# A fused RWKV, attention and mixture-of-experts layer: a subtraction moves from GpSimd to VectorE, the softmax quotient is formed once per tile, the set-up is re-cut, and all order lists are new

## The reference, cut to what matters

```python
def _L0_attn_ref(x, Wk, Wr, Wo, time_decay, time_first):      # x is layer-normed
    k = einsum('btc,hc->bth', x, Wk); v = r = einsum('btc,hc->bth', x, Wr)
    y = wkv_scan(-exp(time_decay), time_first, k, v)          # stable recurrence over t
    return einsum('bth,ch->btc', sigmoid(r) * y, Wo)

def _L0_ffn_ref(x, ...):                                      # x is layer-normed
    h = _rmsnorm(x, gamma1)
    q  = (h @ Wq + bq).reshape(b, t, H, HD)                   # 16 heads of 32
    kv = ((h @ Wdown + bdown) @ Wup + bup).reshape(b, t, H, 2 * HD)
    att = softmax(einsum('bthd,btgd->bthg', q, k) / sqrt(HD)) # over the heads of one token
    out = einsum('bthg,btgd->bthd', att, v).reshape(b, t, D)
    x = x + (out @ Wo + bo)
    h2 = _rmsnorm(x, gamma2)
    gate = softmax(h2 @ Wg + bg)                              # 8 experts, dense
    return x + einsum('btd,edf,bte->btf', h2, We, gate)
```

## Time and profile before

| what | value |
|---|---|
| median of three runs | 2910.02 us (2909.48 to 2913.99) |
| profiled execution, its own time | 2906.95 us |
| its span, first to last instruction | 2905.1 us |
| mean granted TensorE clock | 0.978 |
| TensorE matmul busy | 2618.6 us, 90% |
| VectorE busy | 2453.4 us, 84% |
| ScalarE busy | 1522.6 us, 52% |
| GpSimd busy | 1006.4 us, 35% |

### The profile page before, as it was taken

One profiled execution on the slowest core, in us unless ns is written; L12 is line 12 of the kernel. 1 busy time (PEld: TensorE's weight loads), 2 busy tenths in 40 slices (PEclk: granted clock), 3 DMA queues, 4 the chain that ended last, 5 costly groups with the idle time before them and its releaser, 6 DMA issues.

```text
span 2905.1 us, 49052 instructions
## 1 busy us (share of the span) xinstructions
PE 2618.6 (90%) x18896; PEld 1579.7 (54%) x18896; DVE 2453.4 (84%) x4353; ACT 1522.6 (52%) x2783; POOL 1006.4 (35%) x970
## 2 busy tenths in 40 slices
PE   2447999999999999999999999999999999999899
PEld 2324555555556555555655555555555555565454
DVE  5688888889888888988888898888889888888853
ACT  5664555555555555555555555555555555554531
POOL 0354333334333333433333343333333333333320
PEclk9768999999999999999999999999999999999999
DMA  6011111111111101111110111111011111111110
GB/s 213 15 30 30 38 37 16 29 32 37 38 37 32 21 26 35 37 38 38 23 30 23 38 37 37 37 23 28 26 37 38 38 38 22 26 28 37 30 23 15
DMA packets 579083, 102.51 MB, mean 35 GB/s; under 512 B 547346, under 2 KB 547474, under 8 KB 578834
## 3 DMA queue, kind: packets, MB, share of 16 engines
q1 hardware_dynamic: 578852, 99.39, 16.5%
HBM read 48.49 MB, written 16.78 MB: 22 GB/s over the span
## 4 chain that ended last, share of the span: by engine, by line
PE 54%; DVE 32%; ACT 6%; issue 4%; POOL 2%; SPq 1%; DMA 0%; DVEq 0%; ACTq 0%; POOLq 0%
PE bank L1333 49%; DVE wkv L1134 4%; DVE ks L1219 3%; PE bank L1355 3%; DVE acc L1311 3%; DVE zz L1158 2%; DVE wkv L1123 2%; DVE e L1147 2%; DVE ev L1167 2%; DVE on L1253 2%; DVE zz L1130 2%; DVE mcol L1234 1%; DVE h2t L1096 1%; ACT ot L923 1%; DVE hrow L1225 1%
## 5 line engine op out<-in xcount | busy, mean ns | idle before, releaser
L1333 PE MATMUL bank<-w_e,h2t 128*128 128x512 f16 x6144 | 1392.8, 380 | 72.9 <-DVE acc L1311 52.6
L1333 PEld LDWEIGHTS bank<-w_e,h2t 128*128 128x128 f16 x6144 | 587.3, 98 | 754.6 <-DVE acc L1311 77.1
L1311 DVE SCALAR_TENSOR_TENSOR acc<-bank,gates,acc 128x512 f32<-128x512 f32 x512 | 376.6, 741 | 136.6 <-PE bank L1333 132.3
L727 POOL TENSOR_TENSOR pr<-pr 128x512 f16<-128x512 f32 x256 | 307.1, 1200 | 281.9 <-ACT pr L901 279.2
L899 ACT ACTIVATE pr<-bank,plog,col 128x512 f32<-128x512 f32 x256 | 197.1, 770 | 201.0 <-PE bank L1501 201.0
L1134 DVE TENSOR_TENSOR_SCAN wkv<-e,wkv 128x256 f32<-128x256 f32 x256 | 255.9, 1040 | 22.9 <-ACT e L827 19.6
L696 POOL TENSOR_TENSOR zz<-wkv,zz 128x512 f32<-128x512 f32 x64 | 106.7, 1667 | 432.2 <-DVE ev L1145 432.2
L1333 PE MATMUL bank<-w_o,xo 128*128 128x512 f16 x768 | 176.1, 387 | 49.7 <-DVE xo L1096 49.5
L1158 DVE RECIPROCAL zz<-zz 128x256 f32<-128x256 f32 x128 | 218.5, 1729 | 0.0
L901 ACT ACTIVATE pr<-bank,plog,col 128x512 f16<-128x512 f32 x256 | 197.0, 770 | 0.0
L1333 PE MATMUL bank<-xo,w_k 128*128 128x256 f16 x1536 | 175.6, 275 | 12.0 <-DVE xo L1096 12.0
(11 more groups left out here) (197 smaller groups left out, 4297.7 us busy)
## 6 DMA issues: line engine op xcount, KB each, us to landing
qs<-qo SPq DMA_DIRECT2D x384, 64.0 KB, 2.4
xk<-in_attn_x SPq DMA_DIRECT2D x32, 512.0 KB, 4.8
x<-in_attn_x SPq DMA_DIRECT2D x32, 512.0 KB, 3.9
result<-acc SPq DMA_DIRECT2D x32, 512.0 KB, 2.8
ks<-k SPq DMA_DIRECT2D x128, 64.0 KB, 2.4
w_e<-in_ffn_We SPq DMA_DIRECT2D x7, 1024.0 KB, 14.2
qs<-in_attn_Wk SPq DMA_DIRECT2D x1, 1024.0 KB, 5.8
ks<-in_attn_Wr SPq DMA_DIRECT2D x1, 1024.0 KB, 8.0
```

The costliest lines, as they stand in the source:

```text
L727: nc.gpsimd.tensor_tensor(pr16[:, 1, k % 2, :], pr[:, k % 2, :], pr16[:, 0, k % 2, :], ALU.subtract).then_inc(att_pool.sem, 1)
L1311: V.scalar_tensor_tensor(out=acc[:, s, :], in0=moe_bank[u % 2][:, :], scalar=gates[:, s, e:e + 1], in1=acc[:, s, :], op0=ALU.mult, op1=ALU ...
L1333: ins = nc.tensor.matmul(dst, left(a), right(b), start=(n == 0), stop=(n == last))
```

## The change

It has five parts.

1. The low half of the probabilities is formed by VectorE (`att_plo`) and no longer by GpSimd (`att_scores` of GpSimd is gone). Same operands, same shape, eight times a tile.
2. VectorE's `att_probs` only adds the two halves of a block's result, the column of sums included (33 columns a group, not 32). The reciprocal of all 32 sums and one multiplication of 128x1024 follow once per tile in `fin_back`, each behind a wait on the step before it.
3. In the set-up, the largest absolute values of `o1` and `o2` are found by ScalarE's `set_abs` and no longer by VectorE's `set_max`, and `set_max` for the small weights waits for the first two of them.
4. The loads are one step each in SyncE's list, and the turned weight blocks use six banks.
5. All lists are new.

```diff
-MAXED = ["k", "r", "o1", "q", "o2", "small", "experts"]
+MAXED = ["k", "r", "q", "small", "experts"]
+SUMMED = ["o1", "o2"] + [f"e{e}" for e in range(E)]
+TURN_BANKS = [0, 1, 4, 5, 6, 7]
...
 DVE_ORDER = [
-    ("mix_value", 1, 2), ("mix_scan", 1, 2), ("moe", 3, 4), ("mix_rec", 2, 2), ("moe", 4, 4), ("moe", 5, 4),
-    ("att_probs", 0, 3), ("att_probs", 1, 3), ("mix_rec", 3, 2), ("mix_gate", 1, 2), ("att_probs", 2, 3),
...
+    ("mix_gate", 1, 2), ("att_plo", 0, 3), ("moe", 4, 4), ("att_plo", 1, 3), ("mix_split", 1, 2), ("att_probs", 0, 3),
+    ("att_plo", 2, 3), ("att_probs", 1, 3), ("att_plo", 3, 3), ("att_probs", 2, 3), ("pre_stats", 0, 1),
...
-        on = sb("on", [P, G, HD])
+        on = sb("on", [P, G, HD + 1])
...
         def turned(n):
-            return bank[n % 2][:, :]
+            return bank[TURN_BANKS[n % len(TURN_BANKS)]][:, :]
...
@@ gpsimd
-            def att_scores(t, k):
-                pool.wait_ge(*att_act.done(t, "ex", 2 * k + 1))
-                if k >= 2:
-                    pool.wait_ge(*att_pe.done(t, f"PV{k - 2}"))
-                nc.gpsimd.tensor_tensor(pr16[:, 1, k % 2, :], pr[:, k % 2, :], pr16[:, 0, k % 2, :], ALU.subtract).then_inc(att_pool.sem, 1)
...
@@ scalar
             def set_abs(_, k):
-                name = f"e{k // 2}"
+                name = SUMMED[k // 2]
...
@@ vector
                 if name == "small":
+                    dve.wait_ge(summed, 2 * CB)
                     dve.wait_ge(smalls_in, 16 * 7)
...
                 elif name == "experts":
-                    dve.wait_ge(summed, E * CB)
+                    dve.wait_ge(summed, len(SUMMED) * CB)
...
+            def att_plo(t, k):
+                dve.wait_ge(*att_act.done(t, "ex", 2 * k + 1))
+                if k >= 2:
+                    dve.wait_ge(*att_pe.done(t, f"PV{k - 2}"))
+                V.tensor_tensor(pr16[:, 1, k % 2, :], pr[:, k % 2, :], pr16[:, 0, k % 2, :], ALU.subtract).then_inc(plo_dve.sem, 1)
+
             def att_probs(t, k):
                 pv = att_bank[ATT_BANK["PV", k]][:, 0:4 * VW].rearrange("p (g d) -> p g d", g=4)
-                og = on[:, 4 * k:4 * k + 4, :]
                 if k == 0 and t.back(1):
                     dve.wait_ge(*fin_dve.done(t.back(1), "ot"))
                 dve.wait_ge(*att_pe.done(t, f"PV{k}"))
-                V.reciprocal(rden[:, 4 * k:4 * k + 4], pv[:, :, HD]).then_inc(att_dve.sem, 1)
-                V.tensor_reduce(og, pv.rearrange("p g (l d) -> p g d l", l=2)[:, :, 0:HD, :], AX, ALU.add).then_inc(att_dve.sem, 1)
-                dve.wait_ge(*att_dve.done(t, "norm", 3 * k + 1))
-                V.tensor_tensor(og, og, rden[:, 4 * k:4 * k + 4].unsqueeze(2).to_broadcast([P, 4, HD]), ALU.mult).then_inc(att_dve.sem, 1)
+                V.tensor_reduce(on[:, 4 * k:4 * k + 4, :], pv.rearrange("p g (l d) -> p g d l", l=2), AX, ALU.add).then_inc(att_dve.sem, 1)
...
+                V.reciprocal(rden[:, :], on[:, :, HD]).then_inc(fin_dve.sem, 1)
+                dve.wait_ge(*fin_dve.done(t, "den"))
+                V.tensor_tensor(on[:, :, 0:HD], on[:, :, 0:HD], rden[:, :].unsqueeze(2).to_broadcast([P, G, HD]), ALU.mult).then_inc(fin_dve.sem, 1)
+                dve.wait_ge(*fin_dve.done(t, "quot"))
...
@@ tensor, set_turn
-                    if n >= 2:
-                        pe.wait_ge(lo_done, n - 1)
+                    if n >= len(TURN_BANKS):
+                        pe.wait_ge(lo_done, n - len(TURN_BANKS) + 1)
...
@@ tensor, att_probs
-                pe.wait_ge(*att_pool.done(t, "p_lo", k))
+                pe.wait_ge(*plo_dve.done(t, "p_lo", k))
```

More of the change, by code:

```diff
@@ new lines @@
+    ("mix_decay", 1, 1), ("pre_stats", 0, 2), ("att_latent", 0, 0), ("mix_sum", 1, 1), ("mix_value", 1, 1),
+    ("mix_scan", 1, 1), ("att_stack", 0, 0), ("mix_rec", 2, 1), ("att_vt", 0, 0), ("mix_rec", 3, 1),
+    ("pre_norm", 0, 2), ("att_vlo", 0, 0), ("att_max", 0, 0), ("att_max", 1, 0), ("att_max", 2, 0), ("att_max", 3, 0),
+    ("att_m", 0, 0), ("mix_gate", 1, 1), ("mix_split", 1, 1), ("att_plo", 0, 0), ("att_plo", 1, 0),
+    ("mix_project", 0, 1), ("att_probs", 0, 0), ("att_plo", 2, 0), ("att_probs", 1, 0), ("att_plo", 3, 0),
@@ new lines @@
+    ("pre_stats", 0, 2), ("att_plo", 0, 4), ("att_plo", 1, 4), ("att_probs", 0, 4), ("att_plo", 2, 4), ("moe", 5, 5),
+    ("pre_norm", 0, 2), ("att_probs", 1, 4), ("att_plo", 3, 4), ("att_probs", 2, 4), ("att_plo", 4, 4),
+    ("mix_gate", 1, 3), ("att_probs", 3, 4), ("att_plo", 5, 4), ("mix_split", 1, 3), ("att_probs", 4, 4),
+    ("att_plo", 6, 4), ("att_probs", 5, 4), ("att_plo", 7, 4), ("moe", 6, 5), ("moe", 7, 5), ("mix_project", 0, 3),
+    ("att_probs", 6, 4), ("att_probs", 7, 4), ("mix_turn", 0, 2), ("att_stats", 0, 3), ("moe", 8, 5),
@@ new lines @@
+    ("att_max", 1, 3), ("att_max", 2, 3), ("att_max", 3, 3), ("moe_gate", 0, 4), ("moe", 0, 4), ("att_m", 0, 3),
+    ("pre_stats", 0, 1), ("moe", 1, 4), ("mix_rec", 2, 2), ("mix_rec", 3, 2), ("moe", 2, 4), ("mix_gate", 1, 2),
+    ("att_plo", 0, 3), ("moe", 3, 4), ("att_plo", 1, 3), ("moe", 4, 4), ("mix_split", 1, 2), ("pre_norm", 0, 1),
+    ("att_probs", 0, 3), ("att_plo", 2, 3), ("att_probs", 1, 3), ("att_plo", 3, 3), ("att_probs", 2, 3),
+    ("att_plo", 4, 3), ("att_probs", 3, 3), ("att_plo", 5, 3), ("att_probs", 4, 3), ("att_plo", 6, 3), ("moe", 5, 4),
@@ new lines @@
+    ("att_probs", 5, 3), ("att_plo", 7, 3), ("moe", 6, 4), ("mix_project", 0, 2), ("mix_turn", 0, 1), ("moe", 7, 4),
+    ("att_probs", 6, 3), ("att_probs", 7, 3), ("att_stats", 0, 2), ("att_norm", 0, 2), ("fin_back", 0, 3),
+    ("mix_decay", 0, 1), ("moe", 8, 4), ("moe", 9, 4), ("mix_sum", 0, 1), ("mix_value", 0, 1), ("mix_scan", 0, 1),
+    ("mix_rec", 0, 1), ("att_turn", 0, 2), ("mix_rec", 1, 1), ("mix_gate", 0, 1), ("moe", 10, 4), ("moe", 11, 4),
+    ("mix_split", 0, 1), ("fin_project", 0, 3), ("mix_decay", 1, 1), ("att_latent", 0, 2), ("moe", 12, 4),
@@ new lines @@
+    ("moe", 13, 4), ("mix_sum", 1, 1), ("mix_value", 1, 1), ("mix_scan", 1, 1), ("moe", 14, 4), ("moe", 15, 4),
+    ("att_stack", 0, 2), ("att_vt", 0, 2), ("fin_turn2", 0, 3), ("att_vlo", 0, 2), ("att_max", 0, 2),
+    ("att_max", 1, 2), ("att_max", 2, 2), ("moe_gate", 0, 3), ("moe", 0, 3), ("att_max", 3, 2), ("att_m", 0, 2),
+    ("moe", 1, 3), ("mix_rec", 2, 1), ("moe", 2, 3), ("moe", 3, 3), ("mix_rec", 3, 1), ("mix_gate", 1, 1),
+    ("att_plo", 0, 2), ("att_plo", 1, 2), ("moe", 4, 3), ("moe", 5, 3), ("att_probs", 0, 2), ("att_plo", 2, 2),
@@ L388 @@
+    ("moe_store", 0, 1),
 ]
@@ L624, in set_masks, with set_experts @@
+            def set_experts(_, e):
+                load_weight(f"e{e}")
             def set_masks(_, k):
```

442 lines of the change are left out of this document (210 added, 232 removed).

## The result

The changed kernel takes 2813.01 us in the median of four runs (2812.12 to 2816.03), the kernel before 2910.86 beside it (2909.48 to 2913.99): ratio 0.9664, 95% interval 0.9647 to 0.9681. That is 98 us, more than twice the 41 forecast (2910.86 to 2870). The time is near the low end of the range, and near the 2820 of the first rival.

What follows compares the result with a forecast made beforehand. TensorE was taken to bound the body, working 80.8 of 85.05 us a tile. From 2907 us, 14 for the set-up and 22 for the body came off, 2871, predicted as 2870; range 2808 to 2903.

Steps and rivals of the forecast that it cites:

- the first rival: Body: TensorE nearly saturated; if the lists place VectorE right, 1.5 us idle a tile remain, 2820 us; chance 0.26.
- the body's sum of waits: Body: TensorE's waits fall from 4.35 to 3.5 us a tile, -0.85 a tile, -22 us over 26 tiles.
- acc: Body: TensorE's wait for additions to `acc` falls from 2.03 to 1.1 us a tile, about 1.0 before unit 14.
- h2t: Body: TensorE's wait for the second norm's low half rises from 0.77 to 1.3 us a tile, VectorE starting 0.5 late.
- Banks and xo: Body: waits for probability banks and the recurrence's low half, 0.81 + 0.51 before, become 0.9 us a tile.
- The rest: Body: TensorE's other waits stay at 0.2 us a tile.
- The floor: Body: TensorE's 80.8 us of work a tile stays unaltered; only its 4.3 us idle can be gained.
- VectorE's sum: VectorE per tile: +5.5 subtraction, -3.7 and +1.6 quotient, -4.6 less disturbance: -1.2 us, or +0.8 by the other bound.
- The relief of 4.6: VectorE beside the probabilities: instructions no longer stretched by GpSimd's L727 save 4.6 us a tile, bounds 2.6 and 4.6.
- Set-up and fill: Before the body: -14 us, first projection near 98 us; the fill's new order costed at nothing, could take back all 14.
- the six banks take no wait away: Set-up: six banks for turning remove no wait on the path, as turning is done before 46 us either way.
- The third: Rival, slower: subtraction in VectorE's in-order queue makes it late, 2933 us, or GpSimd disturbs it, 8 us a tile; 0.10 for both.

Runs made afterwards that it cites:

- old_lists_quot: Kernel before with its own lists and GpSimd's low halves, only the quotient formed once per tile instead of per block: 2859.4 us, ratio 0.9813.
- new_lists_only: Changed kernel with the probabilities' low halves back on GpSimd and the quotient per block, keeping new lists and set-up: 2843.2 us, ratio 0.9766.
- plo_pool: Changed kernel with only the probabilities' low halves back on GpSimd; new lists, quotient per tile and set-up stay: 2840.6 us, ratio 0.9758.
- old_lists_none: Kernel before with its own lists, the probabilities' low half a constant zero that no engine subtracts: 2832.6 us, ratio 0.9731.
- new_lists_none: Changed kernel with the probabilities' low half a constant zero that no engine subtracts: 2793.7 us, ratio 0.9596 to the kernel before.
- old_lists_both: Kernel before with its set-up and old lists, low-half subtractions inserted on VectorE and the quotient once per tile: 2966.6 us, ratio 1.0188.
- new_lists_extra: Changed kernel plus eight GpSimd subtractions a tile whose result nobody reads: 2862.7 us, ratio 0.9834 to the kernel before.

## Why the prediction was right or wrong

- **The step that failed** is the body's sum of waits, 3.5 us a tile left of 4.35, on a busy time of TensorE taken as fixed. It gave -0.85 a tile, -22 us; measured are -3.1 a tile, -80 us: 2.4 of idle and 0.7 of busy time. Every term of the 3.5 was too large. acc: 1.1 forecast, 18.2/23.2 tiles = 0.8 measured, at unit 14 as said. h2t: 1.3, measured 0.76, which is what it was before: the half microsecond of lateness did not come. Banks and xo: 0.9, measured 0, with 0.43 for the low half instead. The rest: 0.2, measured 0. Measured together: 1.98. With the set-up the forecast came to -36 us, the profiled execution measured -91.
- **What the runs show behind it.** Two things. In the old lists the reciprocal and the multiplication of each block made the bank and xo late: old_lists_quot clears both waits alone, for 52 us, and without them the two blocks that I counted as late, by 0.6 and 0.3 us, are not late at their banks. And the lists alone give 68 us with set-up, while I let them change VectorE's load by nothing ("Its load stays as it is, near 74 to 76 us"). They take 4.1 us a tile off it (new_lists_only). 3.1 of these are 8 scans by 0.138, 2 products e<-e,v by 0.522 and 2 ev<-e,ev by 0.465 us; after has 71.8. How much of the shorter waits comes from these shorter instructions and how much from the places of the pieces stays open: the load by itself doesn't decide, as plo_pool shows.
- **What bounds the kernel.** Right: TensorE's work bounds the body, and VectorE was late, not overloaded. The floor was wrong. I took 80.8 us of matmuls as fixed and 4.3 us idle as all there is to have. The idle time fell by 2.4 and the busy time by 0.7 (80.70 to 79.98) with the same matmuls. The busy time tends to go with the number of waits: by TensorE's waits of 500 to 2400 us some 6 a tile before (80.70), 4 in old_lists_none (80.19), 3 after (79.98), 2 in new_lists_none (79.79), which would be about 0.2 us for each wait beside the idle time that it shows. It is a correlation with exceptions: new_lists_only has 3 waits a tile too, and 80.37; and the profile models the ends of matmuls. One place fits it: where nothing is waited for, the transposes begin at 1479.19, 0.16 before the modelled end of the units ahead of them (1474.00 + 5.35); with the wait they don't overlap. No run tests it.
- **VectorE's sum.** For the subtraction, the quotient and the relief the sum was right: -1.2 forecast, -0.7 in old_lists_both. The relief of 4.6 was 4.2 in old_lists_none, but one part of it was put down to the wrong instruction: e<-e,v stood beside L709, not L727. The gate, 2 x 0.400 us, which the sum did not have, made up for most of it. The Trainium skill (GPSIMD Engine Reference, Key points) says that GpSimd shares its SBUF interfaces with VectorE and contends with VectorE instructions that have two SBUF inputs or run in a 2-port mode. The traces agree with it for two inputs, beside other GpSimd instructions than the one that I priced too. Without it the sum was +1.7.
- **Set-up and fill.** -14 forecast, -9 measured at tile 3. The first projection came 11.3 earlier, 3 us less than forecast, nearly all of it because ScalarE began with the experts 3.2 us later than I took. Another 2.4 went in the fill, inside the bound of "take back all 14". That the six banks take no wait away was wrong, by 9 us at the first product and about 2 at tile 3.
- **Rivals.** The first, at 0.26, is nearest in size (26 x 2.8 forecast, 26 x 3.1 measured) and in its mechanism, lists that place VectorE's pieces right. That its 2820 is so near is in part luck: the idle time fell by 2.4 and not by 2.8, the busy time, which it left alone, by 0.7, and the set-up gave 9 and not 14. What I held against it, long pieces of VectorE ahead of unit 14 and of h2t, costs 0.8 us each and no more. The third has its mechanism confirmed twice: the subtraction in VectorE's queue by old_lists_both, the disturbance by new_lists_extra; the lists are what keeps the kernel out of it.

How the gain divides, in one order of steps: lists and set-up 68 us (new_lists_only starts tile 3 at 287.97, 7.6 earlier than before, and its body gives 26 x 2.32 = 60, which only the lists can give), the quotient 3, the move 28. In another, the quotient 52 first. Neither division is the true one. Not settled either: how much of old_lists_none's 78 us is the shorter chain of a block and how much the disturbance, and how far better placed subtractions would repair old_lists_both.

## What to carry to other kernels

When work on GpSimd stretches VectorE, look up for each stretched instruction which GpSimd instruction ran beside it, and price an order by what it puts side by side, not only by the sum of durations. Judge removed stalls of TensorE by the period and not by the idle time alone: here the period fell by 3.1 us where the idle time fell by 2.4. When parts of a change attack the same lateness, time each alone in both orders before crediting any of them: the same edit was worth 52 us in the old lists and nothing that can be told apart (3 us and -1 us) in the new ones.

## What the runs showed of the hardware

- A VectorE instruction on 128x2 values with two SBUF inputs took 0.154 to 0.160 us alone and 1.107 to 1.109 while GpSimd worked on 128x512, whether GpSimd's result was used or not (L1112 after, L1130 in new_lists_extra). Even so small a one takes nearly as long as GpSimd's instruction then (1.16 to 1.20 us).
- VectorE's additions to acc, with one operand in a PSUM bank, took 0.735 to 0.747 us in the mean in every kernel, with GpSimd busy 465.5 or 724.8 of 1900 us (after, new_lists_extra), and never more than 0.754: they were not disturbed.
- Two tensor inputs are not needed to be disturbed. `zz<-e,ucol` reads one tensor and a column of scalars; before, it stood beside GpSimd's low halves of the keys (two took 1.42 us from 1433.90 on, GpSimd's L714 ran from 1433.49), after it does not. Stretch 500 to 2400 us of before, then of new_lists_only:

```profile
L1130 DVE TENSOR_SCALAR zz<-e,ucol 128x256 f32<-128x256 f32 x88 | 44.3, 544 | 1.6
```

```profile
L1137 DVE TENSOR_SCALAR zz<-e,ucol 128x256 f32<-128x256 f32 x92 | 28.4, 351 | 1.6
```

- GpSimd is disturbed as well: its subtraction of 128x512 took 1.200 us in the mean before and 1.498 in new_lists_extra, where VectorE's subtractions stand beside it.
